# Two attention layers on one core: loops over units replaced by one written-out pipeline with a ring of three PSUM banks

## The chip, the cores and the metric

One NeuronCore of a Trainium2 chip. The metric is the device time of one execution in microseconds. The kernel of before took 5394.19 us (median of three runs, 5388.27 to 5412.34).

## What is computed

The input is an image batch x of 2 x 128 channels x 56 x 56 pixels (3136 tokens). Two layers follow each other.

Layer 0 is an attention over pooled keys. Each of 8 heads has two halves of 8 channels. A 3x3 average pool with stride 2 gives 784 key tokens. Each half-head has its own softmax of 3136 x 784 scores; the two maps are mixed by weights `pi` that come from the mean query, and multiply the 16 channels of values. The output goes through `w_out` and a batch norm and is added to x:

```python
px = avg_pool_3x3_s2(x)
qt = conv1x1(x, w_qs, b_qs);  kt = conv1x1(px, w_qs, b_qs);  vt = conv1x1(px, w_vs, b_vs)
pi = softmax(mix_w @ qt.mean(2))
attn = softmax(q @ k2 / temperature) * pi        # for each half-head
x = conv1x1(sum over the two halves of attn @ v, w_out) * bn_gamma / sqrt(1 + eps) + bn_beta + x
```

Layer 1 is a full attention, 3136 x 3136 for each of 8 heads of 16 channels, with layer norm over channels in front and a bias that depends on the distance of two pixels alone; that bias comes from a small network of three layers (2, 32, 32, 8) over the 111 x 111 distances:

```python
xn = (x - mean) / sqrt(var + eps) * gamma
q, k, v = split(w_qkv @ xn)
attn = softmax(q @ k.T * scale + bias[None])
x = w_out @ (attn @ v) + x
```

## The kernel before, in words

**Units.** A unit is eight image rows (448 query tokens, `QB`) of one batch for one group of four half-heads (layer 0, 4 groups) or four heads (layer 1, 2 groups). There are 7 units in a group: 56 in layer 0, 28 in layer 1. Keys stand in 7 tiles of 112 (layer 0) or 28 tiles of 128 (layer 1).

**Two passes.** The softmax needs the maximum of each query. Pass 1 (`pass1`, L374 on TensorE, L890 on VectorE) computes the scores of the next unit with queries on partitions, two products at a time (r = 0, 1, on rows 0 to 47 and 64 to 111 of the array) into PSUM banks 4 and 5, and VectorE takes a maximum of each: a plain reduce in layer 0 (L907), an add of the bias and a maximum in layer 1 (L903). Product i waits until VectorE has done with product i - 2 (L381). A unit has 16 pairs in layer 0 and 56 in layer 1. `negate_maxima` (L883) and `turn_maxima` (L456) put the negated maxima, turned by a float32 product with the identity, into row 48 of the stacked queries. Pass 2 (`pass2_scores`, L390) computes scores with keys on partitions, the maximum subtracted by that row, for p = 0, 1 into banks 0, 1 and 2, 3; layer 1 adds the bias by four more products (`pass2_bias`, L404). ScalarE takes the exponential of two banks at once (L707), and `pass2_values` (L413) multiplies by the values, four heads beside each other in bank 6, in float32, with a column of ones that gives the denominator.

**The end of a unit.** ScalarE copies bank 6 to `sums` (L665). TensorE turns the denominators (L430), VectorE takes reciprocals and widens them (L859, L861), TensorE turns them back (L436), VectorE multiplies (L866), TensorE projects out (L442), and VectorE adds into `xacc` (L873, L875). All this shares bank 7.

**Precision of queries and keys.** Each is stacked as high part, high part and rest: TensorE projects in float32 (L448, L468), ScalarE writes the high part in float16 (L669, L683), TensorE subtracts it through a masked product (`mask_q` L451, `mask_keys` L471), and the result is written out again (L673, L928).

**Order.** Every engine runs the same hand-written section (TensorE L487, ScalarE L686, VectorE L948) of 14 or 56 slots, one half-tile each: pass 2 of a unit beside pass 1 of the next, beside the queries of the one after, with the end of the last unit in slots 2 to 5. `Layer.deal` deals the pairs to the slots. Sections stand in loops over the units of a group, and semaphores are taken back to zero by `settle` (L128). Within a group the sections overlap; when a group ends, the next group's keys are projected in slots 0 to 14 of a section and pass 1 is squeezed into the later slots (`following`), and `hand_over_keys` and `hand_over_values` copy them to the second set of tiles that pass 2 reads. When a batch or a layer ends, the pipeline drains (`group(ly, b, None)`) and is filled again with `layer_norm` or `pool_source`, `prepare` and a section of pass 1 alone (L619 to L633).

**The start.** Before layer 0 the whole bias network runs (L359 to L372), 21 rounds of product, ScalarE and VectorE, and the mixture `pi`. SP stores the table and spreads it in DRAM (L269 to L279) during layer 0. In layer 1 SP loads for each unit the bias rows in two halves and the rows for pass 1 in two halves (L282 to L296).

GpSimd does nothing but one iota.

## Time and profile before

| | |
|---|---|
| Runs | 5394.19 us median, 5388.27 to 5412.34 |
| The profiled execution's own time (its span, first to last instruction) | 5439.8 us |
| TensorE busy | 5037.0 us (93%) |
| VectorE busy | 3175.2 us (58%) |
| ScalarE busy | 2479.5 us (46%) |
| GpSimd busy | 0.4 us |
| Mean granted TensorE clock | 0.847 of 2.4 GHz |

The profiled execution is one of its own, 0.8% longer than the median of the others. Busy is the time in which an instruction of the engine is under way. TensorE takes instructions in order, and a wait of one holds up all behind it; PE is its products, PEld its loads of weights. In a timeline, a line stands for instructions of one kind next to each other: start, length of the whole, count. The clock (PEclk) is 1.00 for 2.4 GHz and 0.50 for 1.2 GHz, a value between them a mix. In what follows, the distance between two starts is the time for which an instruction holds TensorE's order; its length is longer, because products overlap.

### The profile page before, as it was taken

The numbers are of one execution on the slowest core, as the hardware profiler recorded it, in microseconds if no ns is written. First come the engines' busy times: TensorE is split into PE (matmuls) and PEld (weight loads), VectorE is DVE, ScalarE is ACT, GpSimd is POOL, SyncE is SP. The second block draws the span as 40 slices with busy tenths as digits, with TensorE's granted clock in tenths as the row PEclk, the third lists the DMA queues.
The fourth block names the chain that finished last, engine by engine and source line by source line (L and its number), as shares of the span: only waits on it lengthen the run. The fifth ranks groups of instructions, "written<-read, shape, count | busy, mean of one in ns | idle before, by whom it ended". The sixth has DMA issues, their size and how long they took to land. (4 is left out here: it accounts for less than half of the span.)

```text
span 5439.8 us, 77005 instructions
## 1 busy us (share of the span) xinstructions
PE 5037.0 (93%) x29794; PEld 1670.3 (31%) x29794; DVE 3175.2 (58%) x9067; ACT 2479.5 (46%) x3102; POOL 0.4 (0%) x5
## 2 busy tenths in 40 slices
PE   5999989979989999889999999999899999999999
PEld 2333333323333333322232323223223223222322
DVE  5445555545555545476667576665476666566662
ACT  2334444434444444425555545555435555355555
POOL 0000000000000000000000000000000000000000
PEclk8567776766677766769999999999789999899999
DMA  5999000000000000111221122222022122112211
GB/s 70 48 51 48 3 0 3 0 16 0 3 0 3 0 3 0 27 46 47 70 69 51 45 70 70 54 61 70 4 82 70 47 68 73 47 47 70 69 47 36
DMA packets 241868, 216.34 MB, mean 40 GB/s; under 512 B 200688, under 2 KB 201488, under 8 KB 240912
## 3 DMA queue, kind: packets, MB, share of 16 engines
q1 hardware_dynamic: 239664, 205.84, 21.1%
q10 hardware_dynamic: 2016, 7.96, 0.5%
q8 instruction: 122, 2.00, 0.2%
q14 instruction: 66, 0.54, 0.0%
HBM read 209.98 MB, written 25.99 MB: 43 GB/s over the span
## 5 line engine op out<-in xcount | busy, mean ns | idle before, releaser
L707 ACT ACTIVATE probs<-P 128x896 f32<-128x896 f32 (+1 forms) x2352 | 2074.0, 915 | 1904.4 <-PE P L408 1232.5
L903 DVE CUSTOM_DVE_ANT_0 junk<-P,mstage 112x448 bf16<-112x448 f32 x3136 | 1828.6, 622 | 812.3 <-PE P L388 810.1
L388 PE MATMUL P<-keys_one,q_one 48*112 48x448 f16 (+1 forms) x4928 | 1505.4, 430 | 184.6 <-DVE maxes L907 92.2
L907 DVE TENSOR_REDUCE maxes<-P 112x1 f32<-112x392 f32 x1792 | 929.8, 561 | 787.4 <-PE P L388 780.1
L417 PE MATMUL P<-probs,vals 128*17 128x448 f32 (+1 forms) x9408 | 1282.9, 621 | 5.8 <-PEq L131 5.5
L388 PEld LDWEIGHTS P<-keys_one,q_one 48*112 48x112 f16 x4928 | 517.4, 137 | 1531.6 <-DVE maxes L903 676.8
L399 PE MATMUL P<-q_two,keys 49*128 49x448 f16 (+1 forms) x4704 | 963.8, 400 | 19.1 <-PEq L131 17.9
L408 PE MATMUL P<-bstage,flip 112*56 112x448 f16 x6272 | 894.5, 365 | 0.0
L399 PEld LDWEIGHTS P<-q_two,keys 49*128 49x128 f16 (+1 forms) x4704 | 285.7, 116 | 1007.9 <-issue 948.3
L408 PEld LDWEIGHTS P<-bstage,flip 112*56 112x56 f16 x6272 | 211.2, 105 | 327.8 <-issue 327.8
L678 ACT ACTIVATE q_two<-P 128x448 f16<-128x448 f32 x168 | 91.4, 544 | 460.1 <-ACTq L131 454.9
L417 PEld LDWEIGHTS P<-probs,vals 128*17 128x17 f32 (+1 forms) x9408 | 160.9, 98 | 368.7 <-issue 356.5
L903 DVE DVE_READ_ACCUMULATOR2_ANT maxes<- 112x1 f32 x3136 | 260.7, 83 | 0.0
L448 PE MATMUL P<-xsrc,wg 128*128 (+1 forms) x336 | 230.4, 783 | 29.8 <-PEq L131 27.3
L669 ACT ACTIVATE high<-P,wg 128x448 f16<-128x448 f32 x168 | 106.4, 634 | 284.7 <-ACTq L131 282.8
L461 PEld LDWEIGHTS P<-cst,negmax 112*128 112x128 f32 x1344 | 228.9, 241 | 2.5
L461 PE MATMUL P<-cst,negmax 112*128 112x112 f32 x1344 | 222.1, 321 | 0.0
L859 DVE RECIPROCAL rden<-P 112x16 f32<-112x16 f32 x84 | 21.7, 258 | 228.2 <-DVEq L131 228.1
L673 ACT ACTIVATE q_next<-P,wg 128x448 f16<-128x448 f32 x168 | 105.2, 632 | 104.1 <-ACTq L131 103.8
L436 PE MATMUL P<-cst,rwide 112*128 112x112 f32 x672 | 117.5, 330 | 37.7 <-PEq L131 37.5
L928 DVE TENSOR_SCALAR keys_one<-P,kbias 128x448 f16<-128x448 f32 (+1 forms) x88 | 57.5, 662 | 125.9 <-PE P L474 125.3
L442 PE MATMUL P<-scaled,wout 128*128 128x448 f32 x168 | 121.2, 814 | 7.5 <-PEq L131 5.5
(103 smaller groups left out, 1354.4 us busy)
## 6 DMA issues: line engine op xcount, KB each, us to landing
mstage<-g_max SPq DMA_DIRECT2D x56, 1519.0 KB, 8.2
bstage<-g_bias SPq DMA_DIRECT2D x28, 1568.0 KB, 10.3
bstage<-g_bias SPq DMA_DIRECT2D x28, 1519.0 KB, 7.9
g_max<-t_bf SPq DMA_DIRECT2D x16, 673.8 KB
g_bias<-t_hi SPq DMA_DIRECT2D x8, 679.9 KB
g_bias<-t_lo SPq DMA_DIRECT2D x8, 679.9 KB
wg<-in_wg ACTq DMA_DIRECT2D x12, 386.0 KB, 3.6
xacc<-in_x SPq DMA_DIRECT2D x2, 1568.0 KB, 10.9
```

The lines of the kernel that those rows point to most:

```text
L388: mm(o, q_one[rows, p, t * QT:(t + 1) * QT], rhs, start=True, stop=True).then_inc(scores_made, 1)
L399: last = mm(P[0:kr, 2 * p + r, 0:QB], keys[rows, p, kt * kr:(kt + 1) * kr], q_two[rows, p, :], start=True, stop=not ly.biased, skip_group_ ...
L408: last = mm(P[64 * e:64 * e + W, 2 * p + r, 0:QB], flip[:, :], bstage[0:QT, 2 * p + r, at:at + QB], start=False, stop=True, skip_group_che ...
L417: last = mm(P[32 * s:32 * s + HD + 1, 6, 0:QB], vals[0:kr, kt, s, :], probs[0:kr, ly.ring(kt), s, :], start=(kt == 0), stop=(kt == ly.key_ ...
L436: last = mm(P[:, 7, t * QT:(t + 1) * QT], rwide[:, t, :, :].rearrange("q s c -> q (s c)"), ident, start=True, stop=True)
L442: mm(P[:, 7, 0:QB], wout[:, :], scaled[:, :], start=True, stop=True).then_inc(yproj, 1)
L448: mm(P[:, bank, 0:QB], wg[:, QW + 128 * p:QW + 128 * p + 128], xsrc[:, bass.ds(unit * QB, QB)], start=True, stop=False, skip_group_check=T ...
L461: last = mm(P[:, bank, t * QT:(t + 1) * QT], negmax[:, p, t, :], ident, start=False, stop=True, skip_group_check=True)
L669: A(high[:, p, :], P[:, bank, 0:QB], ACT.Identity, bias=wg[:, BQ + p:BQ + p + 1]).then_inc(qhigh, 1)
L707: A(probs[0:kr, ly.ring(kt), 2 * p:2 * p + 2, :], P[0:kr, 2 * p:2 * p + 2, 0:QB], ACT.Exp).then_inc(exp_done[p], 1)
L903: V.tensor_tensor_reduce(out=junk[:, n % 4, :], in0=P[0:QT, 4 + r, 0:QB], in1=bias, scale=1.0, scalar=-3.0e38, op0=ALU.add, op1=ALU.max, a ...
L907: V.tensor_reduce(out=top, in_=P[0:QT, 4 + r, 0:ly.chunk], op=ALU.max, axis=AX.X)\
```

## The change

The file is written anew around one list. Its parts:

1. **One pipeline.** There are no loops and no sections. `UNITS` lists all 84 units of both layers and batches, `STEPS` all of their key tiles (56 x 7 + 28 x 28 = 1176 steps), and every engine's program is written out over `s`, from 14 steps before the first to 16 after the last, each in two halves `a` and `b`. Pass 1 of the next unit runs over the steps of this one without a break at groups, batches or the change of layer. Semaphores only count up; `settle` is gone.
2. **Jobs at fixed places.** `Plan.place_jobs` puts queries, keys, values, turned maxima, output projection, the network's rounds, the mixture and the layer norm's moments at steps.
3. **A ring of three banks.** Pass 1 and all jobs take banks 4, 5 and 6 in turn; a user waits for whoever used the bank three places earlier (`free`). Values accumulate in bank 7.
4. **Layer 0 in 32-row blocks.** Its four half-heads take 24 rows each (25 with the maximum's row) of blocks of 32, in one tile of queries and one of keys: one query projection a unit in place of two, one turning in place of two.
5. **No masked product.** ScalarE writes the high part multiplied by a mask of 0 and -1, and VectorE adds it to the projection when it stacks (`stack`).
6. **Maxima turned in float16**, one instruction for each 112 queries, not two. The maxima are rounded so before they are subtracted.
7. **Normalising through DRAM** by GpSimd's queue in place of three products and a widening copy.
8. **Two sets of keys, values, weights and queries**, used in turn by groups and units; the copies from one set to the other go.
9. **GpSimd** loads and scales weights, pools the second batch and clears tiles. The residual is made by ScalarE; the output is stored unit by unit.

Pass 2's products, exponentials and values, and the maxima of pass 1, stay in number and shape, but for the rows in layer 0. In a step of layer 1 TensorE's order is now: pairs, scores and bias for `a`; pairs, scores and bias for `b`; values of the step before.

```diff
+RING, RING0, PV = 3, 4, 7
+PRE, POST = 14, 16
...
+    def deal_pairs(self):
+        for unit in UNITS:
+            places = [(s, w) for s in range(self.start(unit.i - 1) - 1, BASE[unit.i] - 1) for w in "ab"]
+            for k, what in enumerate(unit.work):
+                self.pairs[places[k * len(places) // len(unit.work)]].append((unit, k, *what))
...
+        for unit in UNITS:
+            i = unit.i
+            at = self.start(i - 1) - 3
+            for p in range(2 if unit.biased else 1):
+                put(at, "b", "q", i, p)
+            if unit.biased:
+                put(BASE[i] - 10 if i > FIRST1 else BASE[i] - 1, "a", "s", i, 0)
+                put(BASE[i] - 1, "a", "s", i, 1)
+            else:
+                put(BASE[i] - 1, "a", "s", i, 0)
+            put(BASE[i + 1] + (8 if i >= FIRST1 else 7), "b", "o", i)
+        for n in range(len(NET)):
+            put(n, "b", "n", n)
...
+def bank_of(job):
+    return RING0 + PLAN.ring[job] % RING
...
+            def normalise(j):
+
+                pool.wait_ge(sums_made, j + 1)
+                pool.dma_start(d_den[:, :], sums[j % 2][HD:128:32, :]).then_inc(den_out, 16)
+                pool.wait_ge(den_out, 16 * (j + 1))
+                pool.dma_start(den[:, :, :], d_den[:, :].rearrange("s (p a) -> p s a", a=TILES)).then_inc(den_in, 16)
+                pool.wait_ge(rden_made, j + 1)
+                pool.dma_start(d_rden[:, :].rearrange("s (p a) -> p s a", a=TILES), rden[:, :, :]).then_inc(rden_out, 16)
+                pool.wait_ge(rden_out, 16 * (j + 1))
+                if j:
+                    pool.wait_ge(scaled_made, j)
+                for s in range(4):
+                    pool.dma_start(rwide[32 * s:32 * s + 32, :], d_rden[s:s + 1, :].broadcast_to([32, QB]))\
+                        .then_inc(rden_in, 16)
+                pool.wait_ge(rden_in, 64 * (j + 1))
+                if j:
+                    pool.wait_ge(yproj, j)
+                G.tensor_tensor(scaled[:, :], sums[j % 2][:, :], rwide[:, :], ALU.mult).then_inc(scaled_made, 1)
...
+            for s in range(-PRE, LAST + POST):
+                inside = 0 <= s < LAST
+                biased = inside and STEPS[s][0].biased
+                for p, w in enumerate("ab"):
+                    if biased:
+                        for pair in PLAN.pairs[s, w]:
+                            first_pass(*pair)
+                    if inside:
+                        scores(s, p)
+                    if biased:
+                        biases(s, p)
+                    else:
+                        for pair in PLAN.pairs[s, w]:
+                            first_pass(*pair)
+                    beside(s, w)
+                if 1 <= s <= LAST:
+                    values(s - 1)
...
+            for s in range(-PRE, LAST + POST):
+                for p, w in enumerate("ab"):
+                    if 0 <= s < LAST:
+                        exponentials(s, p)
+                    if p == 0 and s - 1 in BASE[1:]:
+                        j = BASE.index(s - 1) - 1
+                        act.wait_ge(pv_done, s - 1)
+                        if j >= 2:
+                            act.wait_ge(scaled_made, j - 1)
+                        A(sums[j % 2][:, :], P[:, PV, 0:QB], ACT.Copy).then_inc(sums_made, 1)
+                    beside(s, w)
...
+                for j in (j for j in range(len(UNITS)) if s == BASE[j + 1] + 3):
+                    dve.wait_ge(den_in, 16 * (j + 1))
+                    V.reciprocal(rden[:, :, :], den[:, :, :]).then_inc(rden_made, 1)
```

The reciprocal stands in VectorE's order three steps after the unit's last tile, and the output projection seven (layer 0) or eight steps (layer 1) after it; the first waits for two transfers, the second for two more and GpSimd's product.

## Rows read from the trace of the kernel before

**Rows 1.** The page: busy time of each engine.

```profile
PE 5037.0 (93%) x29794; PEld 1670.3 (31%) x29794; DVE 3175.2 (58%) x9067; ACT 2479.5 (46%) x3102; POOL 0.4 (0%) x5
```

**Rows 2.** Stretches: length, busy by engine, PEclk, DMA share, GB/s.

```profile
83.00:2295.00 2212.00, 1985.96 (x9056) 742.84 (x9056) 1120.06 (x2323) 927.07 (x1209) 0.00 (x0) 0.69 0.22 12
2295.00:5439.80 3144.80, 3018.12 (x20664) 913.80 (x20664) 2015.12 (x6680) 1534.54 (x1866) 0.00 (x0) 0.96 0.22 58
84.00:548.00 464.00, 425.07 (x1794) 156.67 (x1794) 234.49 (x486) 185.60 (x244) 0.00 (x0) 0.64 1.00 49
...
465.70:468.90 3.20, 2.46 (x16) 0.91 (x12) 2.46 (x5) 1.71 (x3) 0.00 (x0) 0.97 1.12 50
473.80:486.20 12.40, 11.41 (x82) 4.92 (x81) 7.68 (x18) 8.68 (x12) 0.00 (x0) 1.00 0.99 50
...
2283.58:2534.34 250.76, 214.91 (x1056) 71.79 (x1058) 170.89 (x527) 83.02 (x112) 0.00 (x0) 0.76 0.22 59
3104.45:3108.92 4.47, 4.18 (x28) 1.13 (x26) 3.47 (x12) 1.72 (x3) 0.00 (x0) 1.00 0.00 0
3275.26:3376.55 101.29, 99.37 (x716) 29.64 (x714) 68.63 (x232) 52.50 (x64) 0.00 (x0) 1.00 0.25 63
```

**Rows 3.** Timeline of steady steps in layer 1: start, us, engine, line.

```profile
3283.34 1.01 PE L448 MATMUL P<-xsrc,wg 128*128 x2
...
3299.97 0.56 PE L408 MATMUL P<-bstage,flip 112*56 112x448 f16 x4
3300.47 0.36 PE L399 MATMUL P<-q_two,keys 49*128 49x448 f16 x2
3300.76 0.56 PE L408 MATMUL P<-bstage,flip 112*56 112x448 f16 x4
3301.26 0.40 PE L388 MATMUL P<-keys_one,q_one 48*112 48x448 f16 x2
3301.58 0.95 PE L417 MATMUL P<-probs,vals 128*17 128x448 f32 x8
3301.69 0.62 DVE L903 CUSTOM_DVE_ANT_0 junk<-P,mstage 112x448 bf16<-112x448 f32 x1 [0.73 <-PE P L388]
3302.24 0.62 DVE L903 CUSTOM_DVE_ANT_0 junk<-P,mstage 112x448 bf16<-112x448 f32 x1
...
3302.46 0.36 PE L399 MATMUL P<-q_two,keys 49*128 49x448 f16 x2
3302.66 0.65 PE L388 MATMUL P<-keys_one,q_one 48*112 48x448 f16 x2
3302.92 0.12 PEld L388 LDWEIGHTS P<-keys_one,q_one 48*112 48x112 f16 x1 [0.32 <-DVE maxes L903]
3303.24 0.56 PE L408 MATMUL P<-bstage,flip 112*56 112x448 f16 x4
```

**Rows 4.** Groups by line: busy, mean ns, idle before and its releaser.

```profile
L707 ACT ACTIVATE probs<-P 128x896 f32<-128x896 f32 x1568 | 1371.1, 915 | 1234.7 <-PE P L408 1232.5
L907 DVE TENSOR_REDUCE maxes<-P 112x1 f32<-112x392 f32 x1792 | 929.8, 561 | 787.4 <-PE P L388 780.1
...
L763 ACT ACT_TABLE_LOAD x2 | 2.6, 1283 | 0.0
```

**Rows 5.** DMA: the SP queue of the page; landing of the weight loads.

```profile
q1 hardware_dynamic: 239664, 205.84, 21.1%
...
DMA to landing us min/median/max: 3.0/3.6/11.1
```

**Rows 6.** Timeline in layer 0, at either level of the clock.

```profile
122.99 2.07 DVE L907 TENSOR_REDUCE maxes<-P 112x1 f32<-112x392 f32 x4 [3.05 <-PE P L388]
...
462.35 1.86 PE L448 MATMUL P<-xsrc,wg 128*128 x2 [0.48 <-PEq L131]
470.22 1.70 PE L417 MATMUL P<-probs,vals 112*17 112x448 f32 x8
474.88 0.95 PE L417 MATMUL P<-probs,vals 112*17 112x448 f32 x8
```

More of the change, by code:

```diff
@@ L141, in sem @@
             return ctx.enter_context(nc.semaphore(name))
-        xsrc = sb("xsrc", [C, N])
+        src = [sb(f"src{b}", [C, N]) for b in range(NB)]
         xacc = sb("xacc", [C, NB * N])
@@ new lines, in turn_maxima @@
+            def turn_maxima(job):
+                _, i, p = job
+                unit = UNITS[i]
+                pe.wait_ge(neg_made[p], 1 + (i - FIRST1 if p else i))
+                free(job)
+                bank = bank_of(job)
+                mm(P[:, bank, 0:QB], eye16[:, :], q_stack[i % 2][:, p, :], start=True, stop=False, skip_group_check=True)
+                for t in range(TILES):
+                    rows = negmax1[:, p, t, :] if unit.biased else negmax0[:, t, :]
+                    last = mm(P[:, bank, t * QT:(t + 1) * QT], rows, ident, start=False, stop=True, skip_group_check=True)
+                last.then_inc(neg_turned, 1)
@@ L844, in _, with network @@
+            def network(job):
+                n = job[1]
+                r, depth = NET[n]
                 dve.wait_ge(net_act, n + 1)
@@ L1095 @@
+            settle_stacks(len(PLAN.order))
 def kernel(**inputs):
```

1506 lines of the change are left out of this document (736 added, 770 removed).

## The prediction

> **What bounds the kernel now.** I read the page first: TensorE is busy for 93% of the span, VectorE for 58%, ScalarE for 46%, GpSimd hardly at all [rows 1]. Since a busy TensorE may also be one that waits inside a stream, I then cut the span by stage [rows 2]. Layer 0 (83 to 2295 us, 56 units of eight image rows) takes 39.5 us a unit, at a mean granted clock of 0.69: TensorE alternates between its two levels, 1.2 and 2.4 GHz. Layer 1 (2295 to the end, 28 units) takes 112.3 us a unit, at 0.96; a steady unit takes 101.3 at 1.00. The difference between 28 steady units (2836) and 3145 is 309 us of starts, changes of group and drains: the start of a batch costs 250.8 up to its second unit's end.
>
> Inside a steady unit of layer 1, one step (a tile of 128 keys for four heads) repeats every 3.27 us, from a first bias stream at 3299.97 to the same one at 3303.24 [rows 3]. The starts give what each piece holds TensorE's order for: bias 0.50 (twice), scores 0.29 when the bias follows, pair of pass 1 0.32 when the values follow, values 0.88, scores 0.20 when a pair on other rows of the array follows, and 0.58 for the second pair, whose second product waits for VectorE to free one of two banks. VectorE starts on a pair 0.43 after it was issued, takes 0.55 for each maximum and frees the bank 0.12 after the next one's start. 28 x 3.27 = 91.6; the other 9.7 us of the unit are projections, masks, turned maxima, denominators and output on TensorE. VectorE works for 68.6 and ScalarE for 52.5 of the 101.3 us. So what ends last is TensorE's order, with its waits.
>
> **The change, part by part.** The sum is against the profile's own time, 5439.8, which is 0.8% above the median of the runs, 5394.19; I scale at the end. About 0.5% is what a measurement here can tell from none.
>
> *Layer 1, a step.* Two pairs, scores and bias twice, values: nothing is removed. In the new order each half is pair 0.20, scores 0.29, bias 0.50, and the values 0.88 follow: 2 x 0.99 + 0.88 = 2.86 [rows 3]. Ring of three: the second product of the second pair, issued at 0.99, needs the bank of the first pair's first product, free at 0.43 + 0.55 + 0.12 = 1.10, and then its weights (0.12): 0.2 of waiting, so 3.05. Exponentials (two of 0.915, 1.83 a step) [rows 4] have 1.2 to spare, VectorE (4 x 0.55) 0.85. Lower end 2.86, upper end 3.27, if the third bank gives nothing.
>
> *Layer 1, the rest of a unit.* Gone: two mask products, the denominator and reciprocal products, half of the turning (float16 in place of two float32 instructions), the hand-over copies. Left: two query projections and the output, 1.0 each, as the projection at 3283.34 [rows 3], and two turnings of about 0.6 (between 0.3, the scores' price for the same columns, and 1.0, a float32 projection's): 4.1. Five extra users of the ring hold up pairs by some 0.4 each: 2. A unit: 85.4 + 4.1 + 2 = 91.5; 28 units 2562.
>
> *Normalising by way of DRAM.* The sums go out to DRAM, come back transposed, VectorE takes reciprocals at a fixed place, and two more legs bring them back to all rows. The trace has no GpSimd DMA and none so small; the nearest are the weight loads, 3.0 us to landing at best and 11.1 beside the spreading of the tables [rows 5]. The second leg has 448 pieces of 16 bytes, 28 for each of 16 engines, at the 77 ns of a packet (21.1% x 16 x 5439.8 / 239664) [rows 5]: 2.2 more. Two legs: 3.0 + 5.2 + 0.7 of issues = 8.9. VectorE reaches the reciprocal some 6.2 us (layer 0) or 6.8 us (layer 1) after the sums' copy, and everything behind it waits, pass 1 first, then TensorE on the ring. I charge 2.7 a unit in layer 0, 1.1 in layer 1, where one microsecond of VectorE's slack covers it: 31. Lower end nothing, if a leg lands in 3.0; upper end two legs of 11.1. The output's place comes seven or eight steps after the unit's end, 19.5 us or more after the sums, against about 18.5 for all four legs and the product on GpSimd: just covered. If that cover goes, TensorE waits in order.
>
> The Trainium skill ("DMA: Bandwidth & Descriptors", section on the anatomy of one DMA) puts about 2.0 us of fixed time on each DMA from GpSimd and says that the wait for the write's receipt is most of it. By that figure a first leg of 2.0 and a second of 4.2 would just fit, and the two charges would go. No run here shows it yet.
>
> *Layer 1, around the units.* Keys and values of three later groups now stand beside steps, not in a squeezed section: 14 x 0.95 + 4 x 1.5 = 19, three times 57. Layer norm of the second batch: 14 products of 1.0 and seven returns between two tables of ScalarE (1.28 each [rows 4], 2.6 a return, half of it under ScalarE's slack): 28. The drain with its four legs, output and last store: 25. Both batch starts go. Layer 1: 2562 + 31 + 57 + 28 + 25 = 2703, against 3145.
>
> *Layer 0, a unit.* At 2.4 GHz the values' eight instructions take 0.95 [rows 6], as in layer 1, and hold 0.88; scores or a pair 0.20 to 0.29 [rows 3], say 0.25. VectorE takes 0.50 a maximum in a stream (four in 2.07, one in 0.56) [rows 4, 6]. With the first pair at 0, scores follow at 0.25, the second pair at 0.50; its second product waits for the first bank (data 0.36, maximum 0.56, release and weights 0.18, so 1.10), the values run to 2.18, the next scores to 2.43, and VectorE works 2.0 of these. 7 x 2.43, two more pairs 1.4, query projection 1.0 (one instead of two, no mask), one turning 0.5, output 1.0, VectorE's own extras 0.5: 21.5. At 1.2 GHz TensorE bounds: values 1.70 for 0.95 and a projection 1.86 for 1.01 [rows 6], products 0.35: 3.2 a step, and 4.6 of extras, 27. Which level? The 12.4 us stretch that is dense with products holds 1.00, 465.7 to 468.9 is thin, and the clock falls behind it; a layer-1 step with three pairs lasts 4.47 us, occupies TensorE's order for 3.2 of them and holds 1.00 [rows 2]. The new step occupies 1.9 of 2.4 and has no chain of masks and denominators in which it goes thin. I take three quarters at the full level: 22.9. With the 2.7 above 25.6; 56 units 1434.
>
> *Around layer 0.* Work starts without the maximum network and table in front (83 us today before layer 0's stretch begins [rows 2]): load 13, pooling 7, keys and queries 10, pass 1 of unit 0 16, turning 2: 48. The network's 21 rounds now stand beside the first steps, 1.7 each: 35. Keys of the first layer-1 group 19, first layer norm 35 (no slack in these short steps), group changes of layer 0 22, mixture, sums and residual 12. While the tables spread (464 us at a DMA share of 1.00 today [rows 2]) legs get longer; between nothing and 17 units x 16 us I take 6 a unit: 100. Layer 0: 48 + 1434 + 35 + 19 + 35 + 22 + 12 + 100 = 1705, against 2295.
>
> **Sum:** 1705 + 2703 = 4408 in the profile's own scale, x 5394.19 / 5439.8 = 4371; I say 4370.
>
> **The rivals.** *Legs fit* (0.12): every leg lands in about 3 us. 151 + 31 + 70 of contention go: about 4120. For it: the best landing of a load fifty times larger. Against: 16-byte pieces.
>
> *The clock of layer 0 stays low* (0.14). The ring makes TensorE pause shortly at every pair, and if this counts as thin, all of layer 0 runs at 27 + 2.7: 56 x 4.1 = 230 more, 4600. For it: 0.69 today. Against: a TensorE that is full at 1.2 GHz is what precedes each rise in the rows. The Trainium skill ("TensorE: Matmul & The Clock Gate", section on a second failure mode) says that cycling through PSUM banks with short idle times makes the clock alternate; by this rule this is the case that would come. The three-pair step, which waits on two banks and holds 1.00, speaks against it.
>
> *Legs of 7 us everywhere* (0.10): 14 for two with their issues, stalls of 7.8 and 6.2 less slack: (56 + 28) x 5 = 420 more, 4790.
>
> *The third bank gives nothing in layer 1* (0.06): 28 x 28 x 0.22 = 172, 4540.
>
> *Slower than before* (0.03): legs at 11.1 in every unit. The four are in one queue with GpSimd's product, so a unit of layer 0 cannot be shorter than about 46: 56 x 46 + 28 x 106 + 271 + 110, some 5900. It decides from about 10 us a leg. Against: 11.1 was seen only beside the spreading.
>
> **How the numbers follow.** The forecast case (some 4200 to 4540) has 0.55, which is what is left beside the rivals. From 4080 to 4720 the range takes in the forecast, the better case, the low clock and the idle bank, and leaves out the longer legs, the slower case and their neighbourhoods, under 0.2. Faster by over 0.5% 0.96, within 0.5% 0.01, slower 0.03.
>
> **What would show it.** Steady units of layer 1 at 91 to 93 us apart (by the copies of the sums); steps of 3.05; a second-pair wait of about 0.2. Units of layer 0 at 24 to 27 after the spreading, 30 or so during it, at a clock of 0.85 or more; VectorE idle before the reciprocal, released by a DMA, 1 to 3 us a unit. First scores of pass 2 near 50 us, the last of layer 0 near 1700. I am wrong if layer-1 units stay near 100, if the clock of layer 0 stays near 0.7, or if TensorE waits at the output projection for GpSimd.

## The result, and where the time went

The changed kernel takes 4915.44 us (median of 5 runs, 4908.29 to 4941.7); its ratio to the kernel before is 0.909, with a 95% interval of 0.904 to 0.914. The forecast was 4370 with a range of 4080 to 4720: the sign was right, the time lies 545 us above the number and 195 above the range. The profiled execution has a span of 4939.7 us. One execution among the experiments, of the kernel before with 64 rows, took 8546.22 us at a granted clock of 0.46; neither it nor any other in a slow state enters a ratio below.

From the page of the kernel after (busy time, then the tenths of 40 equal slices), to be held against [rows 1]:

```profile
PE 4250.2 (86%) x27098; PEld 1111.1 (22%) x27098; DVE 2960.9 (60%) x8660; ACT 2420.8 (49%) x2830; POOL 517.8 (10%) x819
...
PE   7755378888888888799989999999999999999998
...
PEclk6555555555555556669999999999999999999999
DMA  1499910000000020012222222222232222232321
```

The last line but one tells most of the story: layer 0, the first 17 slices, stands at 5 and 6 tenths of full clock (PEclk) from beginning to end, where it stood at 0.69 before [rows 2]. The stages of the same kernel (us, then busy time of each engine with its count, granted clock, DMA share, GB/s):

```profile
45.00:700.00 655.00, 397.59 (x1715) 100.79 (x1716) 255.02 (x518) 202.15 (x249) 80.82 (x117) 0.54 0.72 40
700.00:1300.00 600.00, 499.18 (x2378) 119.27 (x2378) 332.60 (x678) 261.81 (x322) 110.07 (x183) 0.56 0.04 10
...
1900.00:4939.70 3039.70, 2832.84 (x20603) 759.49 (x20595) 2014.73 (x6735) 1692.24 (x1935) 198.69 (x308) 0.94 0.23 61
```

I divide the run at the copy of the sums of the last unit but one of layer 0, since the last unit already has the first pass 1 of layer 1 beside it (72.4 us for it). In the sum of the forecast this dividing point is 1705 - 25 = 1680, what follows is 2728. Measured: 2133.7 and 2806. So 454 of the 532 us (4939.7 - 4408) are missing ahead of this point and 78 behind it. The copies of the sums also give the units: 44.7 to 54.8 us, and one of 80.4, while the tables are spread; 30.3 to 33.6 afterwards, 36 to 38 at a change of group (225.3 for the seven units of a group, 32.2 each), and 36 to 50 in the last five before this point, beside which the keys of layer 1 and the first layer norm are made; in layer 1 90.9 to 92.9 where the clock is at 1.00, 93 to 99 where it dips, 98 to 108 in the units that make the keys of the next group or the second layer norm.

In layer 1 the pipeline does what was forecast. TensorE in a steady step of the kernel after:

```profile
4330.55 0.40 PE L535 MATMUL P<-keys,q_stack 48*112 48x448 f16 x2
4330.78 0.36 PE L554 MATMUL P<-q_two,keys 49*128 49x448 f16 x2
4331.06 0.57 PE L573 MATMUL P<-bstage,flip 112*56 112x448 f16 x4
4331.56 0.50 PE L535 MATMUL P<-keys,q_stack 48*112 48x448 f16 x2
4331.79 0.46 PE L554 MATMUL P<-q_two,keys 49*128 49x448 f16 x2
4332.18 0.57 PE L573 MATMUL P<-bstage,flip 112*56 112x448 f16 x4
4332.67 0.95 PE L588 MATMUL P<-probs,vals 128*17 128x448 f32 x8
4333.55 0.40 PE L535 MATMUL P<-keys,q_stack 48*112 48x448 f16 x2
```

From pair to pair 3.00 us: 1.01 for the first half, 1.11 for the second, 0.88 for the values, where [rows 3] had 3.27. The second pair spreads out by 0.1 instead of waiting 0.32.

The other loss is the chain of normalising: four transfers one after the other, each of which I call a leg. Beside the spreading of the tables (GpSimd's queue of the kernel after; the first leg goes out at 348.45, the product comes at 396.56):

```profile
348.45 0.58 POOL L423 DMA_DIRECT2D d_den<-sums  x1 [5.62 <-ACT sums L837]
361.04 0.73 POOL L425 DMA_DIRECT2D den<-d_den  x1 [12.00 <-DMA d_den<-sums]
371.81 0.71 POOL L427 DMA_DIRECT2D d_rden<-rden  x1 [10.03 <-DVE rden L1061]
383.46 2.00 POOL L432 DMA_DIRECT2D rwide<-d_rden  x4 [10.95 <-DMA d_rden<-rden]
396.56 1.12 POOL L437 TENSOR_TENSOR scaled<-sums,rwide 128x448 f32<-128x448 f32 x1 [11.10 <-DMA rwide<-d_rden]
```

Each leg is waited for 10 to 12 us here, and both ends are felt: VectorE stands before the reciprocal, and TensorE before the output.

```profile
371.26 0.25 DVE L1061 RECIPROCAL rden<-den 112x16 f32<-112x16 f32 x1 [14.94 <-DMA den<-d_den]
```

```profile
397.78 1.83 PE L653 MATMUL P<-scaled,wg 128*128 128x448 f32 x2 [9.98 <-POOL scaled L437]
```

### The profile page after: what moved, and what is told of

It reads as the page before. It is cut to its first block, busy times and chain, and to the rows that moved or that the text cites. A ratio compares the mean times of both kernels' runs of the same rounds, so it can differ in the third digit from the quotient of the medians.

```text
span 4939.7 us, 69414 instructions
## 1 busy us (share of the span) xinstructions
PE 4250.2 (86%) x27098; PEld 1111.1 (22%) x27098; DVE 2960.9 (60%) x8660; ACT 2420.8 (49%) x2830; POOL 517.8 (10%) x819
## 4 chain that ended last, share of the span: by engine, by line
PE 75%; DMA 9%; DVE 8%; issue 5%; ACT 1%; POOL 1%; SPq 0%; POOLq 0%; ACTq 0%; DVEq 0%
PE P L588 23%; PE P L573 14%; PE P L535 12%; PE P L540 6%; PE P L554 6%; PE P L614 4%; DVE maxes L879 4%; DMA d_den<-sums 4%; PE P L558 4%; PE P L653 3%; DMA d_rden<-rden 2%; DVE junk L875 2%; DMA rwide<-d_rden 2%; DVE q_stack L912 1%; DMA den<-d_den 1%
## 5 line engine op out<-in xcount | busy, mean ns | idle before, releaser
L588 PE MATMUL P<-probs,vals 128*17 128x448 f32 (+1 forms) x9408 | 1381.7, 666 | 27.0 <-ACT sums L837 26.8
L540 PE MATMUL P<-keys,q_stack 24*112 24x392 f16 x1792 | 567.7, 513 | 400.6 <-DVE maxes L879 261.4
L535 PE MATMUL P<-keys,q_stack 48*112 48x448 f16 x3136 | 755.9, 408 | 121.8 <-DVE q_stack L912 51.2
L554 PE MATMUL P<-q_two,keys 49*128 49x448 f16 x3136 | 649.0, 358 | 0.0
L535 PEld LDWEIGHTS P<-keys,q_stack 48*112 48x112 f16 x3136 | 281.0, 126 | 1030.8 <-DVE maxes L875 493.3
L540 PEld LDWEIGHTS P<-keys,q_stack 24*112 24x112 f16 x1792 | 178.2, 169 | 685.0 <-DVE maxes L879 492.5
L558 PE MATMUL P<-q_two,keys 25*112 25x448 f16 x1568 | 316.4, 558 | 0.1
L554 PEld LDWEIGHTS P<-q_two,keys 49*128 49x128 f16 x3136 | 216.9, 125 | 31.8 <-ACT probs L757 20.1
L653 PE MATMUL P<-scaled,wg 128*128 128x448 f32 x168 | 128.7, 862 | 102.9 <-POOL scaled L437 102.3
L432 POOL DMA_DIRECT2D rwide<-d_rden x336 | 168.1, 507 | 238.6 <-DMA d_rden<-rden 231.2
```

The lines of the kernel that those rows point to most:

```text
L432: pool.dma_start(rwide[32 * s:32 * s + 32, :], d_rden[s:s + 1, :].broadcast_to([32, QB]))\
L535: mm(o.rearrange("q (a n) -> q a n", n=W), q_stack[unit.i % 2][rows, p, t * QT:(t + 1) * QT], key_columns(unit.group, p, c, rows), start=T ...
L540: mm(o, q_stack[unit.i % 2][rows, 0, t * QT:(t + 1) * QT], keys0[unit.group % 2][rows, c * HALF:(c + 1) * HALF], start=True, stop=True)\
L554: mm(P[:, 2 * p + r, 0:QB], keys[unit.group % 2][rows, p, kt * 128:(kt + 1) * 128], q_two[unit.i % 2][rows, p, :], start=True, stop=False, ...
L558: last = mm(P[0:QT, 2 * p + r, 0:QB], keys0[unit.group % 2][rows, kt * QT:(kt + 1) * QT], q_two[unit.i % 2][rows, 0, :], start=True, stop= ...
L588: last = mm(P[32 * h:32 * h + HD + 1, PV, 0:QB], table[0:kr, kt, h, :], probs[0:kr, s % 3, h, :], start=kt == 0, stop=kt == unit.tiles - 1 ...
```

## The experiments

Each edit is told against the kernel after, or against an earlier experiment that it names. Ratios are to the kernel before in the same comparison; those of different comparisons are set side by side as ratios, since the kernel before gave medians from 5413 to 5459 us in them.

**Theories.** A: layer 0 holds 1.2 GHz because TensorE pauses at the ring. B: because of the kind of product that the new layer 0 uses. For the slow units at the start: the spreading stretches the legs, or it slows something else.

### One and three filling products

Here with three; `fill[0]` is true in the steps of layer 0, except the second of a unit.

```diff
                 for r in range(2):
                     job = ("c", unit.i, k, r)
+                    if r and fill[0]:
+                        for _ in range(3):
+                            mm(P[:, PV, 448:512], mean, cst[:, 0:64], start=False, stop=True, skip_group_check=True)
                     free(job)
```

> In every step of layer 0, from the first unit on, one float32 product of a full 128 x 128 array with 64 columns is put ahead of the second product of each pass-1 pair, where TensorE mostly waits for VectorE to free a bank (none in the step in which ScalarE copies the sums). Its result goes to columns that nobody reads. Theory A (the new layer 0 holds 1.2 GHz because TensorE is too thinly occupied while it waits for the ring): the granted clock between 700 and 1900 rises from 0.56 towards 0.7 to 0.9 and the distance of units falls from 32 to 27 us or less, the whole run by 100 to 280 us, to about 4640 to 4820. Theory B (occupation has no part, the kind of product has): clock stays at 0.55 to 0.6; 16 products of about 0.25 us a unit are mostly in the shade of the ring's waits, so the run is between 0 and 100 us longer, 4915 to 5015.

> The same with three such products at each place, 48 a unit, some 12 us of TensorE a unit at 1.2 GHz, 6 at 2.4. Theory A: the clock goes to 0.85 or more and units to 25 to 29 us, the run to 4600 to 4760. Theory B: the clock stays and the unit grows by what the waits don't cover, 3 to 8 us: 5050 to 5300. If one product raises the clock and three make the run longer than one, the dose is what matters.

Measured: 5351.54 us (0.986, 0.979 to 0.992) and 5964.29 us (1.100, 1.091 to 1.108). The window 710 to 1500, which holds steady layer 0, in the kernel after and then with three of them:

```profile
710.00:1500.00 790.00, 656.89 (x3106) 157.71 (x3106) 436.50 (x890) 343.43 (x422) 147.44 (x246) 0.55 0.05 10
```

```profile
710.00:1500.00 790.00, 761.53 (x3079) 391.24 (x3075) 277.93 (x527) 211.64 (x250) 86.35 (x142) 0.51 0.03 6
```

TensorE is busy for 761.5 of 790 us, against 656.9 in the kernel after, and the clock is 0.51, not higher than 0.55. Theory A falls, and with it the idea that the fill is free: one product a pair made the unit 41 us, some 9 more, over twice the expected 16 x 0.25. A float32 product has two instructions here, each loads its weights in 0.295 us (mean of 538), and the fill holds TensorE's order for 0.62 at the lower level; 14 of them a unit make 8.7.

### The spreading in time with the units

```diff
+                    sp.wait_ge(scaled_made, 3 + 4 * h + half)
                    sp.dma_start(dst, rows).then_inc(spread, 16)
                 for a in range(2):
...
+                    sp.wait_ge(scaled_made, 3 + 4 * h + 2 + a)
                     sp.dma_start(dst, rows).then_inc(spread, 16)
```

> SyncE issues the 32 transfers that spread the tables one by one, each when GpSimd has made the scaled sums of another unit, so that each of them (about 14.5 us) runs in the part of a unit in which no leg is under way. Nothing else changes. Theory A (the legs of normalising stretch to 10 to 12 us beside the spreading, and make its units 52 us long): the ten units between 105 and 639 us fall from 52 to about 33 us each, the run gets 180 to 220 us shorter, about 4700 to 4740. Theory B (the spreading slows the units through something else, as memory traffic of the instructions): units of 36 to 45 us for 32 units, the gain below 60 us, or a loss.

Measured: 4735.33 us, ratio 0.872 (0.866 to 0.878). The dividing point falls from 2133.7 to 1931.7: 202 us, nearly all of the gain (217 between the two profiled executions, 180 between the medians). The legs of a unit in the same stretch:

```profile
355.54 0.59 POOL L425 DMA_DIRECT2D d_den<-sums  x1 [16.18 <-ACT sums L839]
357.59 0.74 POOL L427 DMA_DIRECT2D den<-d_den  x1 [1.47 <-DMA d_den<-sums]
364.82 0.72 POOL L429 DMA_DIRECT2D d_rden<-rden  x1 [6.49 <-DVE rden L1063]
367.24 2.01 POOL L434 DMA_DIRECT2D rwide<-d_rden  x4 [1.70 <-DMA d_rden<-rden]
370.97 1.12 POOL L439 TENSOR_TENSOR scaled<-sums,rwide 128x448 f32<-128x448 f32 x1 [1.72 <-DMA rwide<-d_rden]
```

15.4 us from the first leg to the product, where it was 48.1; the waits for a landing are 1.5 to 1.7 instead of 10 to 12. The same 32 transfers of the same bytes run, one beside each of 32 units.

### No legs

```diff
-                pool.dma_start(d_den[:, :], sums[j % 2][HD:128:32, :]).then_inc(den_out, 16)
-                pool.wait_ge(den_out, 16 * (j + 1))
-                pool.dma_start(den[:, :, :], d_den[:, :].rearrange("s (p a) -> p s a", a=TILES)).then_inc(den_in, 16)
                 pool.wait_ge(rden_made, j + 1)
-                pool.dma_start(d_rden[:, :].rearrange("s (p a) -> p s a", a=TILES), rden[:, :, :]).then_inc(rden_out, 16)
...
+            V.memset(den[:, :, :], 1.0)
...
+            G.memset(rwide[:, :], 0.001)
```

> Leaves out the four transfers of normalising in all 84 units: GpSimd multiplies by a constant, VectorE takes the reciprocals of constants at the same place, without a wait; the output is not normalised. The spreading stays as it is. Theory A (units beside the spreading are bound by the chain of legs): they fall from 52 to 32 us, the run to about 4700; the other units of layer 0 and those of layer 1 lose under 1 us each, since their legs landed in 2 to 3 us. Theory B (as predicted, 2.7 a unit in layer 0 and 1.1 in layer 1 beyond the spreading): 150 us more of gain, 4550. Theory C (the spreading slows something else): the units beside it stay over 40.

Measured: 4691.86 us, ratio 0.864 (0.858 to 0.870). With the spreading left as it is, the dividing point falls to 1931.4, to within 0.3 us of the timed spreading: the contention works through the legs alone, and legs that land in 2 to 3 us cost layer 0 nothing (units of 31.0, 36.5, 31.4, 30.4, 31.7 one by one, and within 0.1 us the same in the other). Layer 1 behind it, between the first and the last copy of its stretch, is 27 us shorter than in the timed spreading (2671 and 2698), 1 a unit; the same layer 1 took 2713 in the kernel after, so some 15 us of this are the scatter of one profiled execution. The run leaves out the division by the denominators.

The timed spreading is the base of all further experiments of the changed kernel.

### Blocks of 64 rows again

```diff
-                        rows = slice(32 * h, 32 * h + 24)
-                        mm(o, q_stack[unit.i % 2][rows, 0, t * QT:(t + 1) * QT],
-                           keys0[unit.group % 2][rows, c * HALF:(c + 1) * HALF], start=True, stop=True)\
+                        rows = slice(64 * r, 64 * r + 48)
+                        mm(o, q_stack[unit.i % 2][rows, p, t * QT:(t + 1) * QT],
+                           keys0[unit.group % 2][p][rows, c * HALF:(c + 1) * HALF], start=True, stop=True)\
                             .then_inc(scores_made, 1)
```

and with it the scores over 49 rows, projections, turnings and keys for each p, and the weights of the kernel before in place of the narrow ones.

> On top of the timed spreading: layer 0 goes back to two tiles with blocks of 64 rows, as in the kernel before (48 and 49 rows of the array in a product of scores, two query projections and two turnings a unit, four key projections a group, no narrow weights). The step's own order stays. If the kind of product decides the clock (24 and 25 rows instead of 48 and 49, dense float32 products fewer), the granted clock of layer 0 comes back to 0.69 or more and the unit goes from 31.8 to about 28; 4735 becomes 4500 to 4650. If not, each unit of layer 0 pays for one more projection (1.83) and turning (about 1): 56 x 2.5 = 140 more, about 4880, with the clock still at 0.57. The part of the change that made one tile of four half-heads is then worth some 140.

Measured: 4714.95 us, ratio 0.871 (0.865 to 0.877), the same as the narrow form's 0.872. But the way is another. The window 710 to 1500:

```profile
710.00:1500.00 790.00, 670.24 (x3380) 215.66 (x3378) 468.98 (x967) 392.52 (x490) 151.03 (x246) 0.76 0.31 25
```

The clock is back at 0.76 (0.57 with narrow blocks in the same window) and pays for the second projection and turning. Where the clock is at its upper level and nothing else is waited for, TensorE's step of this kernel is the forecast one:

```profile
995.94 0.40 PE L557 MATMUL P<-q_two,keys 49*112 49x448 f16 x2
...
997.46 0.95 PE L587 MATMUL P<-probs,vals 112*17 112x448 f32 x8
...
998.34 0.40 PE L557 MATMUL P<-q_two,keys 49*112 49x448 f16 x2
```

2.40 us from scores to scores; the forecast had 2.43. (Other steps at this level take 2.81, where the values wait 0.34 for ScalarE's copy of the sums.) At the lower level the narrow form (the timed spreading) needs 3.73 instead of the forecast 3.2, and the wait for the ring is inside it:

```profile
1037.24 0.63 PE L560 MATMUL P<-q_two,keys 25*112 25x448 f16 x4
...
1038.85 0.57 PE L542 MATMUL P<-keys,q_stack 24*112 24x392 f16 x1 [0.65 <-DVE maxes L881]
...
1039.34 1.70 PE L590 MATMUL P<-probs,vals 112*17 112x448 f32 x8
...
1040.97 0.63 PE L560 MATMUL P<-q_two,keys 25*112 25x448 f16 x4
```

### Long filling products

```diff
+                    for r in range(2):
+                        last = mm(P[0:QT, 2 * p + r, 0:QB], nought[:, 0:QT], q_two[unit.i % 2][:, 0, :],
+                                  start=False, stop=True, skip_group_check=True)
                    last.then_inc(st_made, 1)
```

> On top of the timed spreading: behind each product of scores in layer 0 a float16 product of 128 rows by 112 columns with 448 moving columns and weights of zero is added into the same bank, 28 a unit, 0.37 us each at 1.2 GHz. Filling with short float32 products left the clock at its lower level; if what counts is how much of the array works (rows and columns of the product), this one lifts the clock: the clock of layer 0 goes above 0.8 and units stay near 32 or fall below, 4735 or less. If the level does not hang on it, units grow by up to 28 x 0.37 = 10 us and the run to about 5100 to 5300.

> As the dense wide fill, with weights of 0.0001 in place of zero (it adds a small number to the scores of pass 2, so the output is slightly changed). Units of layer 0 took 43.8 us at a clock of 0.57 with zeros. If it matters whether the array multiplies by something, the clock rises above 0.7 and the run falls from 5273 to under 5000. If not, 5250 to 5290 with the clock at 0.57.

Measured: 5272.7 us (ratio 0.971, 0.963 to 0.980) and, with weights of 0.0001, 5261.01 (one run). The clock is 0.58 and 0.57 in the window 710 to 1500, TensorE busy for 741 of 790 us. Full-array products put between small ones don't lift it (0.57 without them), and whether they multiply by zero makes no difference.

### Two banks in the ring

```diff
-RING, RING0, PV = 3, 4, 7
+RING, RING0, PV = 2, 4, 7
```

> On top of the timed spreading: two banks in the ring instead of three, everything else the same. As predicted, the third bank takes 0.22 off a step of layer 1 (3.27 to 3.05 predicted, 3.00 measured with three): 28 x 28 x 0.27 = 210 more there, steps of about 3.27. In layer 0 at 1.2 GHz the second product of the second pair already waits 0.65 with three banks; with two both later products wait, a step goes from 3.73 to about 4.4: 56 x 7 x 0.7 = 270 more. Together about 5200. If the bank is worth nothing, 4735.

Measured: 5490.19 us, ratio 1.013 (1.008 to 1.019): without the third bank the new pipeline is 1.3% slower than the kernel before. Against the timed spreading 360 us come ahead of the dividing point, 399 behind it. TensorE in layer 1:

```profile
2482.71 0.40 PE L537 MATMUL P<-keys,q_stack 48*112 48x448 f16 x2
...
2483.83 0.39 PE L537 MATMUL P<-keys,q_stack 48*112 48x448 f16 x1
...
2484.38 0.39 PE L537 MATMUL P<-keys,q_stack 48*112 48x448 f16 x1 [0.15 <-DVE maxes L877]
...
2486.26 0.40 PE L537 MATMUL P<-keys,q_stack 48*112 48x448 f16 x2
```

A step takes 3.55, not the 3.27 of before: in the new order nothing long stands between the pairs, each product of the second one waits for a maximum, and only the third bank takes this away, 0.55 a step.

### The values between the halves

```diff
                     beside(s, w)
-                if 1 <= s <= LAST:
-                    values(s - 1)
+                    if (w == "a") == (s < LAST and not STEPS[s][0].biased) and 1 <= s <= LAST:
+                        values(s - 1)
```

> On top of the timed spreading: in layer 0 the values of the step before stand between the two halves of a step instead of behind both. The same products, in another order: while the values run (1.70 us at 1.2 GHz), VectorE takes the two maxima of the first pair, and the 0.65 us wait at the second pair goes. A step of 3.73 becomes about 3.1 to 3.2; 7 x 0.55 x 56 = 215 less, about 4520. If the probabilities of the step before are late at the new place (ScalarE), or VectorE is what bounds the step, only a part of it, 4600 to 4735. The clock should stay where it is if waits have nothing to do with it.

Measured: 4714.89 us, ratio 0.871 (0.866 to 0.875), no difference that can be told. Some units have 30.7 instead of 31.5, others 37.7 instead of 36.4 (a group takes 225.2 in both), and the clock fell with it, from 0.57 to 0.54 in the window 710 to 1500. Between 640 and 1650 TensorE's waits for maxima went down (93.8 to 71.5 us) and so did those for q_stack (51.0 to 6.3), those for the sums' copy up (11.9 to 48.1).

> The wide blocks and the values between the halves together, on the timed spreading. Apart, each stood about 20 us below the timed spreading alone. If the clock of the wide form (0.76 in steady layer 0) holds, and the other order takes away a wait of 0.3 a step at 2.4 GHz, units fall from 31.4 to about 29: 4570 to 4620. If the order thins TensorE's work at 2.4 GHz, the clock alternates more and nothing is gained: 4690 to 4720.

Both edits together: 4621.12 us, ratio 0.851 (0.845 to 0.857), clock 0.80. At the upper level the order does pay.

### Only 24 of the 48 rows

```diff
-                        rows = slice(64 * r, 64 * r + 48)
+                        rows = slice(64 * r, 64 * r + 24)
                         mm(o, q_stack[unit.i % 2][rows, p, t * QT:(t + 1) * QT],
```

> The wide blocks on the timed spreading, but each product of pass 1 reads only 24 of its 48 rows (the rows left out hold the fourth cross term and zeros; the maxima move by rounding only). The number of products, the projections, the turnings, the order: all as in the wide form. If the rows that a product occupies decide the clock, it falls from 0.76 to between 0.57 and 0.7 in layer 0 and units become 33 to 34 us (the narrow form's 31.8 and the extra projection and turning), some 4800 to 4850. If the dense float32 products (one more projection and turning a unit) decide, it stays at 0.76 and the time at 4715.

Measured: 5057.77 us, ratio 0.930 (0.924 to 0.935), 7% above the form with 48 rows. The window 710 to 1500, below that of the 48 rows:

```profile
710.00:1500.00 790.00, 727.47 (x2776) 212.83 (x2774) 393.25 (x794) 330.19 (x403) 117.52 (x189) 0.58 0.34 25
```

The same instructions in the same order with the same columns, at 0.58 instead of 0.76. But the edit also changes how the products overlap. A step at the lower level with 48 rows, from the run with wide blocks, then one with 24:

```profile
702.41 0.62 PE L557 MATMUL P<-q_two,keys 49*112 49x448 f16 x2
702.82 0.53 PE L539 MATMUL P<-keys,q_stack 48*112 48x392 f16 x2
...
706.14 0.62 PE L557 MATMUL P<-q_two,keys 49*112 49x448 f16 x2
```

```profile
1248.23 0.62 PE L557 MATMUL P<-q_two,keys 49*112 49x448 f16 x2
1248.78 0.57 PE L539 MATMUL P<-keys,q_stack 24*112 24x392 f16 x2
...
1252.13 0.62 PE L557 MATMUL P<-q_two,keys 49*112 49x448 f16 x2
```

A pair of 24 rows starts 0.55 us after the scores of 49 rows, one of 48 rows 0.41; the step is 3.90, not 3.73. That is 7 x 0.17 = 1.2 of the 7.8 us by which a unit grew (a group from 215 to 270 us), so most of the rest goes with the clock. Whether it fell for the rows themselves or for the lost overlap, this run can't tell; the next ones can, since there the overlap stays. The narrow form of the change has such small products, of 24 and 25 rows.

### More rows than needed

Pass 1, then the scores, of the wide form; the added rows hold zeros in both operands. The narrow form goes from 24 and 25 rows to 32.

```diff
-                        rows = slice(64 * r, 64 * r + 48)
+                        rows = slice(64 * r, 64 * r + 64)
...
-                        rows = slice(64 * r, 64 * r + 49)
+                        rows = slice(64 * r, 64 * r + 64)
```

> On the timed spreading, narrow form: products of pass 1 and of scores read all 32 rows of their block instead of 24 and 25; the added rows hold zeros. If the number of rows read matters by degrees, the clock of layer 0 rises from 0.57 to 0.6 to 0.65 and the run falls by 20 to 80 us from about 4735; if blocks of 32 rows are too small however full, nothing changes.

> On the wide form with the values between the halves (4621 us, clock of steady layer 0 0.81): products of pass 1 and of scores in layer 0 read 64 rows instead of 48 and 49, the added ones of zeros. The same instructions, the same columns. If rows decide by degrees, the clock goes to 0.9 or more, units from 30.3 to 28, the run to 4480 to 4550. If 48 rows are all that counts, it stays at 4621.

> The same in layer 1 as well. Units of layer 1 that hold 1.00 take 92.2 to 92.9 us, those at 0.93 to 0.96 take 95 to 98; about half of the 28 are such. If rows decide by degrees, all hold 1.00 and 30 to 60 us go beside the run with 64 rows in layer 0 alone. If not, the two are within 15 us.

> 64 rows in both layers and the values of the step before between the halves in layer 1 too. A step of layer 1 is 3.00 us, 2.86 without waits. If its 0.14 is the wait at the second pair, 28 x 28 x 0.1 = 80 us less than with the order of before; if the step is bound by what TensorE issues, the same time; if exponentials come late at the new place, up to 100 longer.

| form (on the timed spreading) | us | ratio (95%) | clock, 710 to 1500 |
|---|---|---|---|
| narrow, 24 and 25 rows | 4735.33 | 0.872 (0.866 to 0.878) | 0.57 |
| narrow, 32 rows | 4755.41 (one run) | | 0.57 |
| wide, 48 and 49 rows, values between | 4621.12 | 0.851 (0.845 to 0.857) | 0.80 |
| wide, 64 rows in layer 0, values between | 4505.08 | 0.829 (0.823 to 0.835) | 0.89 |
| the same in both layers | 4480.65 | 0.825 (0.820 to 0.830) | 0.89 |
| and values between in layer 1 | 4431.77 | 0.817 (0.812 to 0.822) | 0.90 |

The window of the third line, then of the fourth:

```profile
710.00:1500.00 790.00, 669.29 (x3555) 218.67 (x3552) 488.96 (x1020) 413.11 (x517) 157.84 (x258) 0.80 0.29 25
```

```profile
710.00:1500.00 790.00, 651.12 (x3795) 217.50 (x3791) 520.40 (x1086) 437.92 (x549) 165.06 (x269) 0.89 0.31 32
```

The distances inside a step at the upper level are the same with 48 and 64 rows (scores to pair 0.23, step 2.40), so the rows of zeros cost no time and do not change the overlap; they bring 116 us. In layer 1 they are worth little (25 us, inside the intervals): its clock from 2500 to 4200 goes from 0.97 to 0.99. The values between the halves in layer 1 bring 49 us more, with every execution below those of the line above but intervals that overlap; the step stays at 3.01, and the gain stands in most of the units beside which keys are made (98 to 102 us in place of 104 to 107). A fuller narrow block does nothing, so it isn't the sum of rows alone. Rows between 25 and 47 in a 64-row block were not run, so a step at some number of rows isn't excluded either.

### The kernel before with 64 rows, and the projections apart

```diff
-                        rows = slice(64 * r, 64 * r + MAXROW)
+                        rows = slice(64 * r, 64 * r + 64)
...
-                    rows = slice(64 * r, 64 * r + MAXROW + 1)
+                    rows = slice(64 * r, 64 * r + 64)
```

> The kernel before the change, with products of pass 1 and of scores over 64 rows instead of 48 and 49 in both layers, the added rows of zeros; nothing else. If rows decide the clock here as well, layer 0's clock goes from 0.69 to 0.8 or more; its units of 39.5 us, in which TensorE bounds, lose 3 to 5 us, and the run 150 to 300 of 5394: 5100 to 5250. If the clock's alternation there comes from the thin stretches alone, 5394 within 0.5%.

Measured: 5271.26 us (median of three), ratio 0.970 (0.959 to 0.981). The clock in the window 710 to 1500 goes from 0.69 to 0.78 (the kernel before, then this one):

```profile
710.00:1500.00 790.00, 700.12 (x3169) 257.33 (x3168) 395.69 (x815) 325.31 (x424) 0.00 (x0) 0.69 0.01 4
```

```profile
710.00:1500.00 790.00, 683.49 (x3434) 267.02 (x3433) 428.45 (x887) 353.09 (x462) 0.00 (x0) 0.78 0.01 4
```

Of the 171 us between the profiled executions 152 are gone by the last unit but one of layer 0. What rows do is no property of the new pipeline.

```diff
-                put(at, "b", "q", i, p)
+                put(at - (1 - p), "b", "q", i, p)
...
-            before = range(BASE[first.i - 4], BASE[first.i - 2] + UNITS[first.i - 2].tiles - 3)
+            before = range(BASE[first.i - 5 if first.g else first.i - 4], BASE[first.i - 2] + UNITS[first.i - 2].tiles - 3)
```

The edit is shown as it stands in the second of the two runs; in the first the query projections are moved in layer 1 alone.

> On top of the timed spreading: the two query projections of a unit of layer 1 stand one step apart instead of next to each other, and the key and value jobs of groups 9 and 11 are spread over four units instead of three. If the jobs' price in layer 1 (units of 103 to 107 beside 92.5, and waits of TensorE for q_stack and keys of 52 and 44 us in all) comes from users of the ring that stand together, 40 to 60 us go: 4680. If each costs its own 2 us wherever it stands, the sum stays within 15 us of 4735.

> On the fastest form so far (64 rows in both layers, values between the halves, 4432 us): the two query projections of a unit one step apart, in both layers, and the key and value jobs of groups 9 and 11 over four units instead of three. TensorE waits 118 us for q_stack and 33 us for keys in the trace of that form. If users of the ring that stand together make that wait, 50 to 100 us go: 4330 to 4380. If each has its own wait wherever it stands, 4432 within 20.

Measured: on the timed spreading 4724.66 us (0.869, 0.865 to 0.873), no difference; on the fastest form 4387.72 us (0.806, 0.799 to 0.813), some 1% less than 4431.77, with intervals that just overlap. TensorE's waits for q_stack in the latter went up in layer 0 (80.7 to 98.7) and down in layer 1 (37.0 to 23.7), so the gain, if it is one, isn't that wait; the clock of the run is 0.947 against 0.940. This last kernel leaves nothing out; by the two ratios (0.806 / 0.909) it takes 11% less time than the changed one.

## Why the prediction was wrong, step by step

- **The clock of layer 0: the step that failed.** "I take three quarters at the full level: 22.9", reasoned from how much of TensorE's order is occupied. Measured 0.56 (700 to 1300), nearly all at the lower level, and a unit of 32.2 with its share of the group change where the sum has 25.6 + 0.4: 6.2 x 55 = 341 of the 454 us ahead of the dividing point. In the forecast's own terms 4.1 of these 6.2 are the level (27 for 22.9), 4.8 are the low unit, which was itself too short (next point), and 2.7 come off again, because the legs cost layer 0 nothing. The rival "the clock of layer 0 stays low" was there with 0.14 and 4600; its mechanism, pauses that count as thin, is wrong too, and so is the argument against it, that a TensorE full at 1.2 GHz precedes each rise: with the pauses filled it was busy for 761.5 of 790 us and stayed at 0.51. What moved the clock was the kind of product: back to 64-row blocks, from 0.57 to 0.76; from 48 to 64 rows in them, from 0.80 to 0.89. The row on which I relied, the three-pair step that holds 1.00 [rows 2], is made of products over 48, 49, 112 and 128 rows. What I costed as removed work was removed (a projection of 1.7 us and a turning of 0.7 a unit at 1.2 GHz), and its price in clock was as large: with wide blocks the time is the same.
- **The low unit of 27.** Steps of 3.73, not 3.2: the sum let TensorE bound them, while the second product of the second pair waits 0.65 for the ring at 1.2 GHz too. Seven times 0.53 is 3.7 of the 4.8 us; the wait for the stacked queries, 30.0 us between 700 and 1300 or 1.6 a unit, had no term. So the rival of the low clock was undersized too.
- **The step at the upper level.** 2.43 forecast, 2.40 measured where the clock is there. Right.
- **The spreading.** 100 us charged, "between nothing and 17 units x 16"; measured 202, ten units at 53 on average. The upper end held. What I took, 6 a unit, was short: with the 11.1 us of [rows 5] the rival "slower" had a unit of 46, and I didn't apply it to the one stretch in which such landings had been seen. Ten units x (46 - 26) are 200.
- **The legs elsewhere.** 2.7 and 1.1 us a unit charged, 151 in layer 0 and 31 in layer 1. Measured nothing in layer 0, where the charge hid part of the miss in the clock, and 27 us in layer 1, give or take the 15 us of scatter. The second leg, for which I added 2.2 us of small pieces, landed in a median of 2.2. The Trainium skill ("DMA: Bandwidth & Descriptors", anatomy of one DMA on the GpSimd path) has about 2.0 us for each; the uncontended legs, with medians of 1.8 to 2.1 in the timed spreading, agree; those beside the spreading in the kernel after, with medians of 8.3 to 12.7, do not.
- **Layer 1.** 2728 forecast from the dividing point on, 2806 measured. The step is 3.00 (3.05), a unit at full clock 90.9 to 92.9 (91.5 + 1.1). Sizes were off around the units: the eleven units beside which keys of the next group and the second layer norm are made take 119 us more than 92.5 each, against 57 + 28 charged, and eleven others are 1 to 6 us longer, 35 in all, at a clock that dips to 0.93 to 0.98, for which there was no term. (The 28 of the layer norm does not come out of its own parts, 14 + 7 x 1.3 = 23.)
- **The third bank.** 0.22 a step forecast for bank and order together, 0.27 measured (3.27 to 3.00). The bank alone, taken away, costs 0.55, since the new order without it falls behind the old one. The rival that it gives nothing fell.
- **The signs to look for.** Pass 2's first scores came at 47.5 (near 50). The end of layer 0 did not come near 1700. Of the three signs of being wrong two are there: its clock was below 0.7, and TensorE waited at the output projection for GpSimd, 89.2 us in eight waits up to 700. The third, units of layer 1 near 100, holds for their mean (98.0) and not for the steady ones.

What stays open: why the clock answers to the kind of product. More rows in a 64-row block went with a higher clock (24, 48, 64: 0.58, 0.76 or 0.80, 0.89; at 24 the overlap changed too), while more rows in a 32-row block and full-array fills between small products did not raise it.

## What to carry to other kernels

A change that makes each product smaller can lose by the clock what it saves in instructions: compare the granted clock of a stretch before and after, not only the instruction count, and try the same products over more rows, of zeros if need be, since they cost no time here. A chain of small transfers with waits between them must be costed at its contended landing wherever a bulk transfer runs; holding the bulk transfer to the free part of each unit gave 180 us by the medians. A ring's depth and the order of what stands between its users belong together: the order that was faster with three banks was slower than the old one with two.

## What the runs showed of the hardware

- In 64-row blocks the granted clock of TensorE changed with the rows that the products read, at equal columns, counts, order and distances: from 0.80 to 0.89 with 64 in place of 48 and 49, the added ones zeros; in the kernel before from 0.69 to 0.78. With 24 rows in place of 48 in pass 1 it fell from 0.76 to 0.58, but there the overlap changed with it. In 32-row blocks 32 rows in place of 24 and 25 changed nothing (0.57 in both).
- A pair of 24-row products behind scores of 49 rows started 0.55 us after them at the lower level, one of 48 rows 0.41.
- A TensorE that is busy for 96% of a stretch (761.5 of 790 us) can stand at 0.51. The Trainium skill ("TensorE: Matmul & The Clock Gate", the second failure mode) puts an alternating clock, in a kernel that cycles through PSUM banks, down to short idle times between groups of products; here the idle times were filled and the clock did not rise, so the trace doesn't bear this out for layer 0.
- A product over 64 rows takes the same time as one over 48 (0.40 us for two in a row at the upper level in both), and each of the two instructions of the float32 fill (128 x 128) loaded its weights in 0.295 us on average.
- The small transfers of normalising, issued by GpSimd, landed in medians of 1.8 to 2.1 us (by leg) in the timed spreading. In the kernel after, between 45 and 620 us, the medians were 8.3, 9.4, 12.7 and 10.6 us for the four legs, beside a spreading from DRAM to DRAM that kept the DMA engines at a share of 0.97 (150 to 600 us).
